# Expert blocks: the gather of block b+3 goes ahead of the scatter of block b

## The reference

```python
h = h + L1_ffn(layernorm(h))   # and so for L0 to L3, mixer and ffn
```

```python
logits = x @ router
top, idx = top_k(logits, k); share = softmax(top)
for each token t and each of its experts e:
    out[t] += share[t, e] * (act(x[t] @ w_up[e]) @ w_down[e])
# gated ones (layer 3): act(x @ w1[e]) * (x @ w3[e]) in place of act(x @ w_up[e])
```

## Time and profile before

| | |
|---|---|
| median of 3 runs | 2568.31 us (2567.3 to 2573.68) |
| profiled execution | 2570.38 us |
| its span, first to last instruction | 2567.1 us |
| busy share PE / PEld / DVE / ACT / POOL | 79% / 58% / 46% / 35% / 33% |
| mean granted TensorE clock | 0.857 |
| PE idle before line 1924, ended by the gather's DMA | 69.4 us |
| POOL on gathers (169 DMAs) | 168.8 us, 999 ns each |
| POOL on scatters (161 DMAs) | 152.8 and 103.8 us, some 1595 ns each |

### The profile page before, as it was taken

The page is one execution under the profiler, slowest core; times in us unless marked ns, Lnnn a source line. Parts: engine busy times, 40 slices in busy tenths (PEclk is TensorE's granted clock), DMA queues, the critical chain, the costliest instruction groups (busy, mean ns, idle before and its releaser), DMA issues. The chain is left out here.

```text
span 2567.1 us, 42132 instructions
## 1 busy us (share of the span) xinstructions
PE 2017.2 (79%) x13338; PEld 1496.5 (58%) x13338; DVE 1189.0 (46%) x2907; ACT 891.9 (35%) x1860; POOL 845.4 (33%) x759
## 2 busy tenths in 40 slices
PE   9745777987985885885985847777499957999998
PEld 8511223665764774664874312223489946999987
DVE  4348994233552112564112789998422234222222
ACT  1247783133342323343223645553222222122211
POOL 0204551013111444001454056664234412444443
PEclk9758997876986987896997879999699967999999
DMA  7000000000005663003773000000367725777774
GB/s 218 26 0 1 0 0 1 0 0 7 1 9 147 187 170 77 1 0 90 188 202 74 0 1 0 0 0 0 106 179 219 207 71 160 229 224 218 224 204 115
DMA packets 95935, 228.18 MB, mean 89 GB/s; under 512 B 22481, under 2 KB 60948, under 8 KB 87540
## 3 DMA queue, kind: packets, MB, share of 16 engines
q1 hardware_dynamic: 64564, 188.81, 23.1%
q0 software_dynamic: 31296, 38.48, 8.8%
HBM read 199.63 MB, written 27.62 MB: 89 GB/s over the span
## 5 line engine op out<-in xcount | busy, mean ns | idle before, releaser
L1962 PE MATMUL banks<-wt,hid 128*128 128x192 f32 x1932 | 347.5, 337 | 0.0
L1962 PEld LDWEIGHTS banks<-wt,hid 128*128 128x128 f32 x1932 | 328.3, 198 | 0.2
L1937 PE MATMUL banks<-xTblock,wt 128*128 128x256 f32 (+1 forms) x1464 | 267.7, 340 | 1.6 <-ACT xTblock L2020 1.2
L2160 DVE TENSOR_TENSOR hid<-sa,banks 128x512 f32<-128x512 f32 (+1 forms) x183 | 105.8, 578 | 339.2 <-ACT sa L2041 336.3
L2041 ACT ACTIVATE sa<-banks 128x512 f32<-128x512 f32 (+1 forms) x183 | 93.4, 510 | 481.5 <-PE banks L1948 476.6
L1937 PEld LDWEIGHTS banks<-xTblock,wt 128*128 128x128 f32 x1464 | 236.6, 193 | 23.7 <-issue 1.6
L1871 POOL DMA_INDIRECT sums<-yblock,put x96 | 152.8, 1592 | 287.9 <-DVE yblock L2175 177.9
L742 PE MATMUL banks<-g,consts 128*128 128x400 f32 x384 | 184.9, 572 | 60.5 <-DVE g L881 56.4
L1866 POOL DMA_INDIRECT xblock<-table,take x169 | 168.8, 999 | 183.6 <-DVE take L2134 114.2
L850 POOL TENSOR_TENSOR w<-u,spreadB 128x400 f32<-128x400 f32 x192 | 192.7, 1034 | 87.2 <-ACT spreadB L821 87.2
L875 DVE TENSOR_TENSOR_SCAN s<-banks,w 128x400 f32<-128x400 f32 x192 | 188.0, 979 | 4.2 <-POOL w L850 4.2
(11 more groups left out here) (379 smaller groups left out, 3446.4 us busy)
## 6 DMA issues: line engine op xcount, KB each, us to landing
wt<-L3f_packed SPq DMA_DIRECT2D x41, 1152.0 KB, 5.8
wt<-L_packed SPq DMA_DIRECT2D x60, 576.0 KB, 4.8
wt<-L3f_packed SPq DMA_DIRECT2D x41, 576.0 KB, 6.0
wt<-L3m_packed SPq DMA_DIRECT2D x20, 1152.0 KB, 5.8
wt<-L_packed SPq DMA_DIRECT2D x20, 675.0 KB, 5.1
wt<-L3m_packed SPq DMA_DIRECT2D x20, 577.0 KB, 5.8
pixels<-pixels SPq DMA_DIRECT2D x16, 375.0 KB, 5.1
wshift<-w_patch SPq DMA_DIRECT2D x8, 450.0 KB, 12.3
```

Source lines behind the costliest of these rows:

```text
L1937: nc.tensor.matmul(bank[:, n * j:n * (j + 1)], wt[:, v, cols(base, 2 * p + j)], xT[:, v, 0, 0:n], start=(j == 0), stop=False, skip_group_c ...
L1962: last = nc.tensor.matmul(bankY[s], hid[:, m, 128 * s:128 * (s + 1)], wt[:, v, DOWN_AT + DIM * m:DOWN_AT + DIM * (m + 1)], start=(m == 0 a ...
L2160: nc.vector.tensor_tensor(hid[:, 2 * p:2 * p + 2, 0:n], sa[:, (PAIRS * v + p) % 2, 0:2 * n].rearrange("p (m n) -> p m n", m=2), second[:, ...
```

## The change

Only the loop of POOL's program is changed. It starts one step earlier, at b = -1, with a gather alone; each further step first gathers block b+3 (where there is one, the dummy included), and then does for block b what it did before. The waits ahead of a gather move along: the gather of block b+3 overwrites the buffer of block b+1, so it waits until block b+1 has been turned and weighed. The number of gathers, scatters and waits is the same.

```diff
-                for b in range(B):
-                    if b + 2 <= B:
-                        pool.wait_ge(turned, b + 1)
-                        pool.wait_ge(gate_done, b + 1)
-                        gather(b + 2)
+                for b in range(-1, B):
+                    if b + 3 <= B:
+                        pool.wait_ge(turned, b + 2)
+                        pool.wait_ge(gate_done, b + 2)
+                        gather(b + 3)
+                    if b < 0:
+                        continue
                     pool.wait_ge(y_done, b + 2)
                     if b:
                         pool.wait_ge(added[(b - 1) % 2], moved[b - 1])
                         pool.sem_inc(y_free, 1)
                     scatter(b)
```

## The result

The changed kernel takes 2526.24 us (median of 4 runs, 2521.61 to 2530.01) against 2569.01 us (2567.30 to 2573.68) of the kernel before beside it: a ratio of 0.984, 95% interval 0.982 to 0.986. A later group of 5 runs gave 2521.49 against 2566.82, 0.9828 (0.9805 to 0.9850). The forecast was 2518, so about 9 us of the promised 51.7 did not come: 2526.24 lies outside the forecast's own 2512 to 2523, in the part up to 2531 that was added for the first rival; the later group's 2521.49 lies inside it. The profiled execution took 2526.45 us.

What follows compares the result with a forecast made beforehand. Late gathers bound L1 and L2, PE's own work L3m and L3f. Gains of 37.0 and 16.7 us, less 2 for the scatter chain, make 51.7 off 2570.4: 2518 us, own range 2512 to 2523, extended to 2531.

Steps and rivals of the forecast that it cites:

- the promised 51.7: Whole kernel: 53.7 us gained in L1 and L2, less 2 us of returning waits in L1, giving 2518 us.
- the first rival: L1 and L2: scatter chain or full DMA engines bind, losing 7 and 3 us; 2527 us, chance 0.15.
- the late waits: L1 and L2: PE's sixteen waits for gathers after each stage's first, 22.9 and 13.3 us, should all go.
- the slot arithmetic: POOL's list in L1: each gather moved one place earlier lands in time, slack 1.4 to 5.3 us or at least 2.6.
- part of the gain is clock: L1 and L2: matmuls behind late waits run at a lower clock; 17.5 us of the gain.
- the 53.7: L1 and L2 against clean pairs: 37.0 and 16.7 us, of which 36.2 are waits and 17.5 slower matmuls.
- The rival for which the prediction cited the Trainium skill: TensorE's clock stays down without the waits, so only 36.2 us go: 2534 us, chance 0.06.
- L3 has no part: L3m and L3f: PE's own work is the bound, so they stay unchanged within 1 us.
- the added waits: POOL waits for turn and weighing of block b+1 ahead of scatter b: costed at nothing, uncovered 0.3 us a block.
- what is late next: L1's scatter chain, each waiting for the landing before: 14.1 us a turn against 13.37, some 2 us back, bounds 0 and 7.
- 3 us of slack: L1: about 3 of the 5 us that scatters fall behind over seven pairs is absorbed by gathers' slack.
- one of the prediction's own signs of being wrong: Pairs above 14 us in L1; pairs of 13.2 to 13.6 us were expected if right.

Runs made afterwards that it cites:

- two targets: Changed kernel with odd blocks of L1 and L2 scattering into a second DRAM tensor, left out of the output: 2516.70 us, 0.9811 against the kernel before.
- light loads: Changed kernel with weight loads of L1 and L2 cut to 64 columns from the third block on (stale weights): 2515.31 us, 0.9807 against the kernel before.
- the transpositions ahead of the wait: Kernel before, old order, with 16 (L1) or 8 (L2) identity transpositions ahead of each turn of a block of one: 2555.79 us, 0.9964.
- the control: The changed kernel run once more, unaltered: 2521.49 us against 2566.82 of the kernel before, 0.9828.
- the kernel with L1 alone: Kernel before with the new order in L1 only, old order in L2, L3m and L3f: 2535.75 us against 2565.52, 0.9888.

## Why the prediction was right or wrong

**Right: the late waits go.** The sixteen waits of 36.2 us are gone in L2 but for 0.4, and in L1 the first pairs run at 13.37 us; the 5.0 us left in L1 are new waits, after the chain fell behind. One place earlier in POOL's list was enough, as the slot arithmetic had it: where nothing holds the chain (two targets, or light loads) PE waits for the first gather alone.

**Right: part of the gain is clock.** The waits alone account for 36.2 us of the 53.7; the transpositions ahead of the wait bring L1 down by 16.7 us (10 against the shortest L1 of the old order) with the waits' time still spent: added work and remaining waits make 22.0 us where the waits were 22.9. Here the trace agrees with the Trainium skill (TensorE: Matmul & The Clock Gate, section What's actually happening: activity releases the throttle). The rival for which the prediction cited the Trainium skill (same page, section A second HAM failure mode), a clock that swings with small pauses alone, did not occur: the pair with two waits of 0.41 and 0.72 us kept 1.00.

**Right: L3 has no part**, and the added waits on `turned` and `gate_done` cost nothing: L3m and L3f are the same within 1 us, and alone they give 0.9993.

**Wrong in size: what is late next.** The step named the chain of scatters and costed a turn at 14.1 us, the middle of 13.4 and 14.8, which with 3 us of slack made 2 us. A turn is 14.7 to 15.1 us in the slow course, and with it came one of the prediction's own signs of being wrong, pairs above 14 us in L1. The term that was too small is the landing of the scatter of one. It was held at 3.6 us from a single row, and only the landing of the scatter of two was varied; measured, it goes to 5.3 and more once the chain slips. The loss in L1 is 148.99 - 143.0 = 6.0 us in the profiled execution and 7.9 in the control, and none in the kernel with L1 alone. The first rival, at 2527, had the right mechanism in its first half. Its second half, full DMA engines, is refuted by the two-target kernel, and the DMA share of the quick pair was 0.81 and not 0.89. That its 2527 lies so near the measured 2526.24 is in part luck: it had 7 us lost in L1 and 3 in L2, and L2 lost 0.8 (142.43 against 141.58). The rule about ordered semaphore writes (the Trainium skill, DMA: Bandwidth & Descriptors, section Queues, rings and completion order) is in line with landings of 3.5 us without the loads and a median of 5.6 with them; that it is this order and not sharing of the engines no run here separates. The scatter of 3.6 us in the earlier trace rows was no scatter without loads: two were under way when it was issued at 845.87 (landed at 847.13 and 848.54), but none followed until 851.81.

**Not foreseen: the stretches between.** Between L1 and L2 the changed kernel's profiled execution lost 3.7 us, where the instructions are the same. At comparable places after the end of L1 (60 to 80 us), TensorE's clock was 0.77 in the changed kernel,

```profile
1013.91:1033.91 20.00, 18.63 (x264) 13.91 (x257) 10.05 (x22) 6.73 (x15) 0.71 (x2) 0.77 0.01 2
```

and 0.99 in the kernel before:

```profile
1046.72:1066.72 20.00, 17.77 (x289) 13.14 (x281) 12.24 (x28) 9.05 (x18) 1.07 (x3) 0.99 0.00 1
```

The clock of the changed kernel rose from 1.2 to 2.4 GHz some microseconds later. The kernel with the new order in L2 alone, whose L1 has the old order, does the same:

```profile
1044.97:1064.97 20.00, 18.63 (x258) 13.70 (x250) 10.02 (x22) 7.03 (x17) 0.71 (x2) 0.79 0.01 2
```

There this stretch took 233.9 us. With the old order in L1 it took 230.5 to 233.9 us in four traces, with the new one 232.8 to 241.2 in six, so the 3.7 us need no price of the new order; that there is none at all is not shown. The sum was also made from one execution: L1 in the old order took 181.5 us there, but 180.2 and 175.0 in two other traces, and the kernel before ranged from 2553.7 to 2575.5 us in the last group.

Together: the chain cost 4 to 6 us more than forecast. In the profiled execution some 1.5 us of that were made up, since the rest of L1 gained 38.5 us and not 37.0; so L1 is 2.5 us short of its forecast and L2 0.7. The other stretches and L3f lost some 6 us more, with the same program or no late wait there, and that is within what they and the kernel before swing by.

A version that keeps two targets and adds them up later was not built: by the length of L1 its gain would be 6 to 8 us at most (143.05 against 148.99 and 150.94), from which the merging would have to be paid.

## What to carry to other kernels

When a wait is taken out, write down the next loop of waits with all of its terms, and vary every term that shares the DMA engines, not only the largest: a loop that just keeps up can slip into a place where its own transfers take longer, and in both traces of this change it stayed there. A late transfer ahead of TensorE can cost more than its idle time, when the matmuls behind it run at the lower clock. In a queue that waits for a landing, instructions between the issue and the wait are free as long as they fit into the wait, and the same instructions between the wait and the next issue are paid in full.

## What the runs showed of the hardware

A scatter with add of 128 rows of 768 bytes landed a median of 3.5 us after its issue when the weight loads were cut to 64 columns, and in 3.4 to 8.9 us (median 5.6 and 5.7 in L1 of the changed kernel's two traces) among weight loads of 576 and 675 KB. With 2 us of transpositions of a constant ahead of a wait of 0 to 0.9 us, the eight down projections behind it in L1 ran at 4.07 us; with waits of 2.0 to 3.7 us and no such work, 19 of 24 took 5.2 to 6.8 us.
